# Attention and a mixture of experts: tokens sent to their two experts by indirect transfers, the experts' tiles computed inside the attention

## The chip, the cores and the metric

The kernel runs on one core of a Trainium2 chip. The metric is the device time of one execution in microseconds. The engines are PE (TensorE, with weight loads listed as PEld), DVE (VectorE), ACT (ScalarE), POOL (GpSimd) and SP (SyncE, which issues all DMAs of the kernel before). Each has its own instruction stream and they meet by semaphores.

## The reference, cut to what matters

The input x is 2 x 2048 tokens of 256 features, all float32. `xn = layernorm(x)`, and the output is `x + attention(xn) + experts(xn)`.

The attention has 16 heads of 16 features, rotary embedding of Q and K, a causal mask, softmax, and an output projection with a bias.

The experts: gate logits over 10 gates (8 true experts and 2 null ones), softmax, the two largest gates; of these the weights of true experts are divided by their sum; each expert is a 256 x 256 matrix with a bias:

```python
gate_probs = softmax(x @ gate_w.T + gate_b)
weights, selected = top_k(gate_probs, 2)
true_weights = weights * (selected < 8)
norm_w = true_weights / (true_weights.sum() or 1)
out = einsum('te,teh->th', combine_w, einsum('td,edh->teh', x, expert_w) + expert_b)
```

So a token needs at most two of the eight expert products.

## The kernel before, in words

`build` (L1495) calls three parts, each a block in which all engines run and at whose end they meet: `project`, `attend` and `output`. `acc` holds x, then the sums, for all 32 tiles of 128 tokens in SBUF.

**`project` (L61).** Eight steps of one chunk of 512 tokens each (two batches by four chunks, `s = 2 * j + b`). For each chunk DVE computes the statistics (`norm_a`, L388) and normalises (`norm_c`, L399); PE transposes the chunk (`transposes`, L655); ACT writes it as a float16 high half (`copy_xT`, L298) and DVE the low half (`low_x`, L408). Products then run in three float16 passes (high x high, high x low, low x high; `product`, L662). PE makes V and the gate logits (`values`), four blocks of Q and K (`queries`) and, for every token, all eight experts (`experts`, L703: 4 banks a tile, 6 matmuls of 512 columns each). DVE weighs and adds the expert products into `acc` (`combine`, L552). The gate (`gates_a`, `gates_b`, L497 and L507) is a chain of some 40 small DVE operations a chunk. Q and K blocks are copied by ACT (`copy_q`, L321), shuffled and multiplied by DVE (`rope`, L480), multiplied and added by POOL (L270, L272), and split in halves by ACT (`high`, L330) and POOL (`rest`, L275). SP stores V (4 DMAs) and Q and K (16 DMAs) of each chunk to scratch in HBM. Queues are in program order; the first chunk runs in float32 products, so that it need not wait for the split weights.

**`attend` (L777).** Eight groups of four heads (two loop turns unrolled into `r = 0, 1`). Before the first group, PE and DVE work through `first_items`, row maxima for two chunks. In a group there are 40 units (a chunk of 512 queries against a tile of 128 keys). For a unit PE makes scores of four heads in the three banks of psS (`scores`, L1358), ACT takes the exponential (L1215), POOL masks it where it is a diagonal unit (16 of the 40, L1186), and PE multiplies by V (`pv`, L1379). At most 4 units of probabilities are open. Beside this run "items" that use one of the two slots of psP in strict turn: "q", scores for the row maxima of later chunks, reduced by DVE (L1325, L1252); "m", the transposed maxima, which SP stores into Qs (`store_m`, L1105); "o", a chunk's output, transposed by PE (L1425) and normalised by DVE (`normalise`, L1257). The order of scores, items and products on PE is written out by `schedule` (L890), which simulates PE, ACT, DVE and POOL with fixed costs; the same order is used in all groups but the last, which has fewer items. All engines follow it strictly.

**`output` (L1435).** For each of 32 tiles PE transposes the attention's result and multiplies by Wout, ACT copies in between, DVE adds to `acc`, and SP stores 4 tiles at a time.

## Time and profile before

| | us |
|---|---|
| median of 3 runs | 1189.08 (1187.52 to 1189.19) |
| the profiled execution | 1192.72 |
| its span, first to last instruction | 1190.6 |
| PE busy | 1071.2 (90%) |
| DVE busy | 976.3 (82%) |
| ACT busy | 712.0 (60%) |
| POOL busy | 212.7 (18%) |
| mean granted TensorE clock | 0.941 |

The span is some 2 us shorter than the execution's time. Busy shares are means over the three parts, which have different limits; the rows below take them apart. Matmuls are pipelined and their ends modelled, so that a busy PE is not PE at its peak. The clock is a share of 2.4 GHz; its two levels are 1.0 and 0.5.

### The profile page before, as it was taken

To read this page: it belongs to the slowest core of one execution; us is meant where nothing else is said; L and a number is where in the kernel's file an instruction comes from. 1 tells how busy PE (TensorE), PEld (TensorE's weight loads), DVE (VectorE), ACT (ScalarE), POOL (GpSimd) and SP (SyncE) were. 2 spreads that over 40 slices of the span, in tenths; PEclk is the share of its full clock that TensorE was granted. 3 is DMA by queue.
4 is the path that set the end of the run, shared out by engine and by line. 5 is a ranking of instruction groups with operands and counts; after the bars stand their busy time and mean duration, and the time that the engine had idled before them with its cause. 6 is when DMAs were issued, how large, how long until landed. Compare 5 with 4: busy or idle time off the path is not lost. (4 is left out here: it accounts for less than half of the span.)

```text
span 1190.6 us, 25362 instructions
## 1 busy us (share of the span) xinstructions
PE 1071.2 (90%) x7800; PEld 416.2 (35%) x7800; DVE 976.3 (82%) x1610; ACT 712.0 (60%) x1545; POOL 212.7 (18%) x250
## 2 busy tenths in 40 slices
PE   4599899899965999999899999899999999999988
PEld 3244444444421332333323333233333233233247
DVE  6988788788859899999799899889989889989113
ACT  2333232332200688788588788678878868878752
POOL 2534254234510001001001101100100100110100
PEclk9799899899985799999899999989999999999889
DMA  8012122121230401101100200200110110000003
GB/s 292 25 56 80 36 74 67 53 88 36 64 85 13 99 2 45 47 2 46 48 2 11 81 2 2 71 22 3 45 46 2 45 47 2 2 2 2 1 18 124
DMA packets 50207, 53.37 MB, mean 45 GB/s; under 512 B 5201, under 2 KB 40602, under 8 KB 50074
## 3 DMA queue, kind: packets, MB, share of 16 engines
q1 hardware_dynamic: 50074, 51.75, 14.4%
q8 instruction: 65, 1.06, 0.4%
q14 instruction: 68, 0.56, 0.2%
HBM read 30.43 MB, written 20.97 MB: 43 GB/s over the span
## 5 line engine op out<-in xcount | busy, mean ns | idle before, releaser
L1215 ACT ACTIVATE probs<-psS 128x512 f32<-128x512 f32 (+3 forms) x1280 | 586.0, 541 | 216.8 <-PE psS L1367 207.4
L1252 DVE TENSOR_REDUCE blk<-psP 128x2 f32<-128x1024 f32 (+2 forms) x576 | 636.2, 1159 | 64.9 <-PE psP L1328 53.2
L1367 PE MATMUL psS<-Qs,Ks 50*128 50x512 f16 (+3 forms) x1280 | 347.5, 358 | 14.9 <-ACT probs L1215 9.0
L1325 PE MATMUL psP<-Ks,Qs 48*128 48x512 f16 (+3 forms) x1280 | 295.9, 368 | 43.3 <-DVE blk L1252 21.5
L1392 PE MATMUL psO<-probs,Vs 128*32 128x512 f32 (+3 forms) x2560 | 308.7, 554 | 1.4 <-ACT probs L1215 0.4
L1186 POOL TENSOR_SCALAR_AFFINE_SELECT probs<-probs 128x512 f32<-128x512 f32 x128 | 81.5, 636 | 711.7 <-ACT probs L1215 711.7
L666 PE MATMUL psM<-wp,xp 128*128 128x512 f16 x768 | 183.8, 391 | 15.8 <-DVE odd L571 9.8
L1367 PEld LDWEIGHTS psS<-Qs,Ks 50*128 50x128 f16 x1280 | 100.5, 95 | 258.5 <-ACT probs L1215 200.7
L1325 PEld LDWEIGHTS psP<-Ks,Qs 48*128 48x128 f16 x1280 | 74.9, 95 | 169.6 <-DVE blk L1252 128.3
L666 PEld LDWEIGHTS psM<-wp,xp 128*128 128x128 f16 x768 | 75.8, 101 | 111.8 <-issue 19.1
L1328 PE MATMUL psP<-later,eye 64*128 64x128 bf16 x1024 | 95.4, 231 | 0.0
L1392 PEld LDWEIGHTS psO<-probs,Vs 128*32 128x32 f32 x2560 | 51.8, 108 | 87.6 <-issue 73.9
L1328 PEld LDWEIGHTS psP<-later,eye 64*128 64x128 bf16 x1024 | 73.3, 102 | 18.6 <-issue 5.0
L270 POOL TENSOR_TENSOR swp<-swp,trig 128x512 f32<-128x512 f32 x32 | 42.5, 1327 | 180.7 <-DVE rot L486 180.7
L563 DVE SCALAR_TENSOR_TENSOR acc<-psM,cs,acc 128x256 f32 (+1 forms) x128 | 60.7, 474 | 14.1 <-PE psM L666 8.5
L334 ACT CAST part<-rot 128x512 f16<-128x512 f32 x32 | 19.0, 616 | 72.9 <-POOL rot L272 72.9
L1261 DVE RECIPROCAL rs<-psP 128x16 f32<-128x16 f32 x32 | 8.2, 257 | 51.9 <-PE psP L1425 51.9
L327 ACT ACTIVATE qs<-psQ 128x512 f32<-128x512 f32 x28 | 16.6, 593 | 57.2 <-PE psQ L666 57.2
L571 DVE SCALAR_TENSOR_TENSOR odd<-psM,cs,odd 128x256 f32<-128x256 f32 x96 | 45.3, 471 | 0.0
L272 POOL TENSOR_TENSOR rot<-rot,swp 128x512 f32<-128x512 f32 x32 | 41.6, 1300 | 2.5
L666 PE MATMUL psQ<-xp,wqp 128*128 128x512 f16 x168 | 40.9, 379 | 0.0
L277 POOL TENSOR_TENSOR part<-rot,part 128x512 f16<-128x512 f32 x32 | 39.7, 1248 | 6.5 <-ACT part L334 6.5
(115 smaller groups left out, 643.1 us busy)
## 6 DMA issues: line engine op xcount, KB each, us to landing
v_scratch<-vst SPq DMA_DIRECT2D x32, 256.0 KB, 3.2
qk_scratch<-part SPq DMA_DIRECT2D x128, 64.0 KB
Vs<-v_scratch SPq DMA_DIRECT2D x16, 512.0 KB, 4.5
acc<-x SPq DMA_DIRECT2D x8, 512.0 KB, 7.4
Ks<-qk_scratch SPq DMA_DIRECT2D x32, 128.0 KB, 2.7
Qs<-qk_scratch SPq DMA_DIRECT2D x32, 128.0 KB, 2.7
out<-acc SPq DMA_DIRECT2D x8, 512.0 KB, 2.9
we_sb<-we SPq DMA_DIRECT2D x8, 256.0 KB, 7.3
```

The lines of the kernel that those rows point to most:

```text
L270: step(nc.gpsimd.tensor_tensor(swp[k][:, :], swp[k][:, :], trig[:, 1, :], ALU.mult))
L272: nc.gpsimd.tensor_tensor(rot[k][:, :], rot[k][:, :], swp[k][:, :], ALU.add).then_inc(sum_ok[k], 1)
L563: nc.vector.scalar_tensor_tensor(out=rows, in0=psM[:, n, 0:D], scalar=cs[b][:, t, e:e + 1], in1=rows, op0=ALU.mult, op1=ALU.add).then_inc( ...
L571: ins = nc.vector.scalar_tensor_tensor(out=odd[t % 2][:, :], in0=psM[:, n, D:2 * D], scalar=cs[b][:, t, e + 1:e + 2], in1=odd[t % 2][:, :] ...
L666: ins = pe.matmul(out, lhs(x, w, k), rhs(x, w, k), start=(n == 0), stop=(n == len(todo) - 1))
L1186: nc.gpsimd.affine_select(out=v, in_=v, compare_op=ALU.is_ge, fill=0.0, base=0, pattern=[[0, HG], [1, P]], channel_multiplier=-1).then_inc ...
L1215: nc.scalar.activation(probs[u % NPR][:, h, q0:CH], psS[:, n % SB, q0:CH], ACT.Exp, scale=exp_scale).then_inc(s_read[n % SB], 1)
L1252: nc.vector.tensor_reduce(out, src, AX.X, ALU.max).then_inc(item_ok[slot], 1)
L1325: ins = pe.matmul(psP[:, slot, at:at + w], Qs[r][rows, qt // CT, p, t * P:(t + 1) * P], Ks[r][rows, kc, p, 0:w], start=True, stop=True)
L1328: ins = pe.matmul(psP[:, slot, at + w - P:at + w], eye[all_rows, i, :], later[all_rows, i, :], start=False, stop=True, skip_group_check=True)
L1367: pe.matmul(psS[:, n % SB, q0:CH], Ks[r][rows, kt // CT, p, kt % CT * P:(kt % CT + 1) * P], Qs[r][rows, c, p, q0:CH], start=True, stop=Tru ...
L1392: ins = pe.matmul(psO[h * VW:(h + 1) * VW, q0:CH], Vs[r][:, kt, h * VW:(h + 1) * VW], probs[u % NPR][:, h, q0:CH], start=(kt == 0), stop=e ...
```

## The change

**Projection.** The expert products, `combine` and the per-chunk gate are gone. All eight chunks now run one scheme: wait for the split weights, then `values`, `transposes` of the next chunk, four `queries` in two psQ banks. `xn` is kept for all 32 tiles. The low half of Q and K is computed by DVE (`split`) instead of POOL. SP, ahead of the stores, fills the scratch arrays `xs` (9984 rows of 256 float32) and the end of `ys` with zeros. After the last chunk the gate of all 4096 tokens is computed at once, with matmuls that count how many tokens go to each expert and where each token's row lies in a list sorted by expert and padded to tiles of 128; the weights of each expert are split and stored to `we_s`.

**Attention.** In groups 0 and 1 POOL sends the rows of `xn` to their two places in `xs`, two transfers after every mask. In groups 2 to 5 (`kind == "experts"`) nine pairs of tiles a group are worked as items "x" and "y" in the psP slots. In groups 6 and 7 POOL fetches the results from `ys` into `xn`, and DVE adds them, weighed, to `acc` in group 7.

**Output.** The expert biases and `bout` come in by one more product a tile, of a 54-row bf16 matrix of weights with a 54-row matrix of biases.

The core of the diff:

```diff
+            sp.dma_start(xs[:, :].rearrange("(n p i) d -> p n (i d)", p=P, i=2),
+                         zero[...].to_broadcast([P, TRASH // (2 * P) + 1, 2 * D])).then_inc(spare, 16)
...
+            def split(s, k):
+                dve.wait_ge(high_ok[k], ONE + s + 1)
+                nc.vector.tensor_tensor(part[k][:, 1, :], rot[k][:, :], part[k][:, 0, :], ALU.subtract
+                                        ).then_inc(split_ok[k], 1)
...
+            def body(j, start, last):            # DVE, projection
+                for b in range(NB):
+                    s = 2 * j + b
+                    if not (last and b == 1):
+                        low_x(s + 1, 1 - b)
+                    if not (start and b == 0):
+                        split(s - 1, 2)
+                    rope(s, j, 0)
+                    if not (start and b == 0):
+                        split(s - 1, 3)
+                    rope(s, j, 1)
+                    if not last:
+                        norm_a(s + 2, j + 1, b)
+                    rope(s, j, 2)
+                    split(s, 0)
+                    rope(s, j, 3)
+                    split(s, 1)
+                    if not last:
+                        norm_c(s + 2, j + 1, b)
...
+            for e in range(EXPERTS):             # ACT, after the loop; DVE follows with the low half
+                if e >= 2:
+                    act.wait_ge(e_stored[e % 2], ONE + 16 * (e // 2))
+                    act.wait_ge(el_ok, ONE + e - 1)
+                nc.scalar.activation(wep[e % 2][:, 0, :, :], we_sb[:, :, e * D:(e + 1) * D], ACT.Copy,
+                                     scale=wscale[:, OF_E:OF_E + 1]).then_inc(eh_ok, 1)
...
+        EG = MTILES_USED // 2 // 4               # 72 tiles, 9 pairs in each of four groups
+        def with_e(queue):
+            seq, every = list(queue), len(queue) // EG
+            for i in range(EG):
+                at = seq.index(queue[i * every + 2])
+                seq.insert(at, ("x", i))
+                seq.insert(at + 4, ("y", i))
+            return seq
...
+            def load_e(buf, n):                  # SP
+                sp.dma_start(xt[buf], xs[bass.ds(n * 2 * P, 2 * P), :]...).then_inc(e_in[buf], 16)
+                for i in range(2):
+                    e = sp.value_load(etab[0:1, bass.ds(n * 2 + i, 1)], min_val=0, max_val=EXPERTS - 1)
+                    sp.dma_start(wt[2 * buf + i], we_s[bass.ds(e, 1), :, :]...).then_inc(e_in[buf], 16)
...
+            def scatter(t, i):                   # POOL
+                if (t, i) != (0, 0):
+                    pool.wait_ge(scattered, 16 * (TILES * i + t))
+                nc.gpsimd.indirect_dma_start(out=xs[:, :], out_offset=bass.IndirectOffsetOnAxis(ap=idx[:, i, t:t + 1], axis=0),
+                                             in_=xn[:, t, :], in_offset=None).then_inc(scattered, 16)
+            for r in range(2):
+                for d, u in enumerate(masks):
+                    mask(0, r, u)
+                    for t in range(d * EACH, (d + 1) * EACH):
+                        scatter(t, r)
...
+            for d, u in enumerate(masks):
+                mask(3, 0, u)
+                for t in range(d * EACH, (d + 1) * EACH):
+                    gather(t, 0)
+            for d, u in enumerate(masks):
+                mask(3, 1, u)
+                for q in [q for q in range(QUARTERS) if SECOND[q] == d]:
+                    pool.wait_ge(added, ONE + q + 1)
+                    for t in range(q * QT, (q + 1) * QT):
+                        gather(t, 1)
...
+                        elif x[0] in "xy":       # ACT, in the order of the items
+                            if x[0] == "x":
+                                nc.scalar.activation(xT[buf][:, 0, :], psP[:, slot, 0:CH], ACT.Copy, scale=XSCALE
+                                                     ).then_inc(hi_ok, 1)
+                            else:
+                                act.wait_ge(y_stored[buf], ONE + 16 * before)
+                                nc.scalar.copy(yt[buf], psP[:, slot, 0:CH]).then_inc(item_ok[slot], 1)
...
+            def low(j, r, x, slot):              # DVE
+                dve.wait_ge(hi_ok, ONE + EG * (2 * (j - 1) + r) + x[1] + 1)
+                nc.vector.scalar_tensor_tensor(out=xT[buf][:, 1, :], in0=psP[:, slot, 0:CH], scalar=XSCALE,
+                                               in1=xT[buf][:, 0, :], op0=ALU.mult, op1=ALU.subtract
+                                               ).then_inc(item_ok[slot], 1)
+            def add(i, q):
+                dve.wait_ge(y_in[i][q], 16 * QT)
+                for t in range(q * QT, (q + 1) * QT):
+                    ins = nc.vector.scalar_tensor_tensor(out=acc[:, t, :], in0=xn[:, t, :], scalar=wsel[:, i, t:t + 1],
+                                                         in1=acc[:, t, :], op0=ALU.mult, op1=ALU.add)
...
+            def expert(buf, slot):               # PE, 12 matmuls of 256 columns
+                todo = [(w0, w1, k) for w0, w1 in ((0, 0), (0, 1), (1, 0)) for k in range(KC)]
+                for t in range(2):
+                    for n, (w0, w1, k) in enumerate(todo):
+                        ins = pe.matmul(psP[:, slot, t * D:(t + 1) * D], xT[buf][:, w0, at:at + P],
+                                        wt[2 * buf + t][:, of:of + D], start=(n == 0), stop=(n == len(todo) - 1))
...
+                pe.matmul(ps[:, t % 4, 0:D], cT[t % 2][:, :], b54[:, :], start=False, stop=True).then_inc(o_ps, 1)
```

## Rows read from the trace of the kernel before

**Rows 1.** Busy us of each engine by stretch, clock, DMA share, GB/s.

```profile
54.00:343.00 289.00, 260.76 (x1228) 123.96 (x1228) 241.55 (x708) 83.55 (x166) 107.54 (x87) 0.96 0.19 59
343.00:392.00 49.00, 25.12 (x147) 8.51 (x148) 39.26 (x43) 0.00 (x0) 3.69 (x14) 0.52 0.23 59
492.00:584.00 92.00, 85.40 (x757) 28.91 (x757) 82.11 (x93) 71.69 (x160) 10.06 (x16) 0.98 0.10 27
1050.00:1106.00 56.00, 53.33 (x476) 17.42 (x473) 49.75 (x59) 45.59 (x95) 4.46 (x7) 1.00 0.01 2
1106.00:1149.00 43.00, 37.48 (x242) 9.78 (x238) 1.88 (x7) 32.43 (x77) 6.36 (x10) 0.88 0.00 1
1149.00:1190.00 41.00, 36.83 (x192) 30.91 (x192) 13.96 (x33) 11.82 (x32) 0.00 (x0) 0.96 0.31 103
```

**Rows 2.** Timeline of POOL, masks of two groups: start us, us, operation, idle before.

```profile
399.85 0.64 POOL L1186 TENSOR_SCALAR_AFFINE_SELECT probs<-probs 128x512 f32<-128x512 f32 x1 [48.73 <-ACT probs L1215]
...
491.87 0.64 POOL L1186 TENSOR_SCALAR_AFFINE_SELECT probs<-probs 128x512 f32<-128x512 f32 x1 [10.70 <-ACT probs L1215]
...
551.70 0.64 POOL L1186 TENSOR_SCALAR_AFFINE_SELECT probs<-probs 128x512 f32<-128x512 f32 x1 [6.18 <-ACT probs L1215]
...
572.64 0.64 POOL L1186 TENSOR_SCALAR_AFFINE_SELECT probs<-probs 128x512 f32<-128x512 f32 x1 [3.17 <-ACT probs L1215]
```

**Rows 3.** Timeline of DVE and PE in the projection's loop.

```profile
175.88 1.40 DVE L392 BATCH_NORM_STATS2 stat<-acc 128x6 f32 x4
...
177.63 1.29 DVE L413 SCALAR_TENSOR_TENSOR xp<-xnT,xp 128x512 f16<-128x512 f32 x2
...
183.24 1.38 DVE L404 TENSOR_SCALAR xn<-acc,mv,rstd 128x256 f32 x4
...
186.97 0.73 DVE L485 STREAM_SHUFFLE swp<-qs 128x512 f32<-128x512 f32 x1
187.60 0.67 DVE L486 TENSOR_TENSOR rot<-qs,trig 128x512 f32<-128x512 f32 x1
...
301.98 1.46 PE L666 MATMUL psQ<-xp,wqp 128*128 128x512 f16 x6
```

**Rows 4.** POOL's first rotation (timeline) and ACT's high halves (groups of instructions).

```profile
27.87 1.26 POOL L270 TENSOR_TENSOR swp<-swp,trig 128x512 f32<-128x512 f32 x1 [17.50 <-DVE rot L486]
...
L334 ACT CAST part<-rot 128x512 f16<-128x512 f32 x29 | 17.3, 616 | 67.1 <-POOL rot L272 67.1
```

**Rows 5.** Timeline: one DVE product beside POOL and without it.

```profile
40.70 1.15 POOL L277 TENSOR_TENSOR part<-rot,part 128x512 f16<-128x512 f32 x1 [5.05 <-ACT part L334]
...
40.72 1.18 DVE L545 TENSOR_TENSOR c<-cw,den 128x32 f32<-128x32 f32 x1
...
202.44 0.19 DVE L545 TENSOR_TENSOR c<-cw,den 128x32 f32<-128x32 f32 x1
```

**Rows 6.** V stores, issue and landing (min/median/max), and the loads' rate (by stretch).

```profile
L212 SPq DMA_DIRECT2D v_scratch<-vst x32: 372/417/1441, 21.0 to 300.5; - x32
...
DMA to landing us min/median/max: 2.5/3.2/5.3
...
14.00:16.00 2.00, 2.00 (x8) 1.89 (x9) 1.90 (x9) 1.11 (x3) 0.00 (x0) 1.00 1.09 384
```

**Rows 7.** Timeline of DVE in the opening: maxima and low halves of expert weights.

```profile
19.77 4.47 DVE L444 TENSOR_REDUCE whalf<-we_sb 128x2 f32<-128x2048 f32 x2
...
32.10 4.75 DVE L470 SCALAR_TENSOR_TENSOR wp<-we_sb,wscale,wp 128x512 f16<-128x512 f32 x4
```

**Rows 8.** Timeline of DVE and PE inside group 1.

```profile
551.89 4.62 DVE L1252 TENSOR_REDUCE blk<-psP 128x2 f32<-128x1024 f32 x4 [0.22 <-PE psP L1325]
...
555.98 0.65 PE L1425 MATMUL psP<-identf,ot 128*128 128x128 f32 x4
...
565.10 0.26 DVE L1261 RECIPROCAL rs<-psP 128x16 f32<-128x16 f32 x1 [0.81 <-PE psP L1425]
...
574.53 0.43 PE L1392 MATMUL psO<-probs,Vs 128*32 128x128 f32 x8
```

1170 lines of the change are left out of this document (651 added, 519 removed).

## The prediction

> **What bounds the kernel now.** I read the busy time by stretch first. It splits the 1190.6 us span into projection (0 to 343), the attention's opening (343 to 392), eight groups, and the output stage from 1149 [rows 1]. In the projection's loop PE is busy 261 of 289 us and DVE 242: both hold the pace, and ACT (84) and POOL (108) do not. A steady attention group lasts 92.0 us, the distance of its first mask from that of the group before [rows 2]. In it PE is busy 85 to 89, DVE 82, ACT 72, POOL 10. So the projection has two engines near their limit, and the change takes most of the work off both. The groups have PE and DVE near the limit and ACT behind them, and the change puts work on all three. In the last 43 us of attention DVE is all but idle (1.9 busy).
>
> **The projection, from 343 us to what.** Removed are 32 x 4 expert products of 6 matmuls, the DVE sums that follow them, and 8 chains of small gate operations. What is left per chunk on DVE, by the starts in the rows, which overlap a little [rows 3]: the x split 1.2, statistics 1.75, reciprocal and normalise 0.2 + 1.4, four shuffles of 0.63 and four rotary products of 0.6 (4.9), and now also four low halves taken over from POOL, priced as the rotary product, 2.4. Sum 11.9 us. PE: 24 value products of 266 columns, 24 query products of 512 (1.46 us for six, [rows 3]) and 8 transposes, about 10 us. ACT: 4 query copies of 0.6, 4 high halves of 0.616 [rows 4], two x halves and three V and gate copies, about 8. POOL: 8 products of 1.26 [rows 4], 10.1.
>
> DVE is then the longest, but not alone. Two things add. First, the last DVE operation of a chunk (normalise for the chunk after next) is followed by PE transposes (0.6 for the first half), the ACT half (0.6) and two handovers before DVE can go on: 1.5 idle. Second, DVE and POOL can't both read SBUF pairs: the same 128x32 product took 0.19 us with POOL idle and 1.18 beside a POOL subtraction of 1.15 that began 0.02 before it [rows 5]. Eight such DVE operations meet eight POOL operations in each chunk; laying them out one after another gives about 3 us more. I take 16.5 us a chunk. Ends: 14 (no collisions) and 20.
> The Trainium skill's page "SBUF — State Buffer" (section "SBUF: two separate sides") says the pair of ports shared by VectorE and GpSimd is an exclusive lock, taken by a DVE operation with two SBUF inputs for its whole length against a GpSimd operation. By that rule the chunk is 16.5, without it 13.5, 20 us less over the loop; the two rows agree with the rule.
>
> POOL's first rotation starts at 27.9 [rows 4], so DVE began the first shuffle at 26.5. Now the weights' three halves are made first on ACT and DVE (about 2.1 more after overlap) and the value and query products run in three fp16 passes, perhaps at the lower clock (4.4 more): 33 us. Then a fill of scratch with zeros is queued before the first stores: 9984 rows of 1 KB and 768 more, 11.0 MB. The loads reached 384 GB/s [rows 6], say 350: the 9.2 MB of loads end at 28, the fill at 60. The stores of chunk 0 are behind it and land there plus about 3; part[0] is wanted again at 33 + 16.5 + 5 = 55. Stall 8 us (0 to 20). Six chunks of 16.5 and one without normalisation (13) bring the last chunk's first product to 33 + 8 + 99 + 13 = 153, its end (POOL's four rotations) to 168.
>
> Behind the loop stands a serial tail that nothing covers. Gate: 17 operations on 256 or 320 elements per partition, 0.42 to 0.5 each by scaling from the rotary product, about 8; 20 small ones of 0.2, 4; the maxima of the expert weights 4.5 [rows 7] and 0.6; two low halves 1.3; scales 1; waits for 32 counting matmuls and then 33 more at half clock, 4; places and tile table 6.5. Sum 30. Then eight weight splits through two buffers: DVE 1.2 each [rows 7], issue and landing of the 256 KB store 3.2 [rows 6], ACT 0.65 and handovers, 5.9 for each pair of experts, 24 for four. 168 + 54 = 222. The projection gives back 343 - 222 = **121 us** (ends 105 and 140). The attention's opening stays 49.
>
> **Groups 2 to 5: 36 pairs of tiles, nine a group.** A pair is an item "x" (4 transposes, ACT high half, DVE low half) and an item "y" (12 matmuls, ACT copy). Both take one of two psP slots that alternate strictly with the score reductions, 1.15 us each on DVE (four in 4.62, [rows 8]). PE: 0.6 for the transposes (0.65 for four, [rows 8]), and 12 x 256 columns are the columns of the six in rows 3, 1.3 to 1.46; 1.95 x 9 = 17.6 us. DVE: 0.69 of work (the x split's half, [rows 3]), and idleness: in "x" the slot passes 0.65 + 0.6 + handovers and ACT's queue (ACT is 78% busy) while DVE has only 1.15 in the other slot, so 1.0 idle; in "y" DVE sees neither slot for 1.46 + 0.6 - 1.15 and then waits again for the refill, 1.4. Nearest row: DVE stood 0.81 idle ahead of an "o" item, which has no ACT step inside it [rows 8]. 3.1 x 9 = 28 us on DVE, of which its present 10 us of idleness may take some. Below: 14 (both hide in each other); above: 33 (PE's strict order adds waits). I take 23, between PE's 17.6 and DVE's 28: 4 x 23 = **+92** (56 to 132). The transfers, 1 MB a pair, need 3 us of every 12.8 at 350 GB/s; hidden. SP's waits for "y" stand in front of mask-row and next-group loads, but these are wanted several items later.
>
> **Groups 0 and 1: scatters.** After each mask POOL issues two indirect transfers, each waiting until the one before has landed. Queued behind them is the next mask, and for that waits psO's product on PE and all behind it. No row shows an indirect transfer. Landing of a 256 KB store, issue included: 2.5 to 5.3, median 3.2 [rows 6]; an issue costs SP 0.42 to 1.44 [rows 6], and for POOL I take the length of its product, 1.26. Mask, landing and second issue: 0.64 + 3.2 + 1.26 = 5.1 us (ends 0.64 + 2.5 + 0.42 = 3.6 and 0.64 + 5.3 + 1.44 = 7.4). The last eight masks of a group span 20.9 us [rows 2]: 7 x 5.1 - 20.9 = 14.8 late, less the 1.3 between a mask's end and its product [rows 2, 8]: 13 a group, **+26** (6 to 70; at 7.4 the masks ahead of these are late too).
> The Trainium skill's "DMA: Bandwidth & Descriptors" (section "Anatomy of one DMA — SWDGE (gpsimd) path") gives 2.0 us plus bytes over 436 GB/s for a transfer issued by GpSimd, 2.3 here; by it the step would be 4.2 us and the sum for both groups 14 instead of 26. No row here shows it.
>
> **Groups 6 and 7: gathers and sums.** In group 6 the gathers wait for nothing: 0.64 + 2 x 1.26 = 3.2 a mask, 7 x 3.2 is 22, nothing late. In group 7 four bursts of eight hold POOL 10 us each, and 32 DVE sums of 0.4 (by size from the rotary product; 12.8) fall into a stretch in which DVE is busy 50 of 56 us [rows 1]; the other 32 lie where it is idle. **+12** (3 to 30).
>
> **Output.** 32 tiles are 192 matmuls in 36.8 us of PE, almost all of the 41 [rows 1]. One bf16 transpose and one 256-column product more, with their weight loads: 0.25 x 32 = **+8** (4 to 12); the added ACT copy fits.
>
> **Sum.** -121 + 92 + 26 + 12 + 8 = +17. The profiled execution took 1192.7 us beside its span of 1190.6, so it becomes 1210; the median before is 1189.1, so the forecast is **1206 us**.
>
> **Rivals.** *Experts mostly hidden, faster.* No stall by the fill (-129), a group gains only 17 (PE's own addition: 68), scatters 10, gathers 6, output 6: -39, 1150 us. For it: PE's busy time in rows 1 counts latencies that overlap, and DVE has 10 us idle. Against: two slots only, strict order. 0.31. *POOL is the bound in groups 0 and 1 and in 7*: step 7.4, scatters 70, gathers 30: +79, 1268. It decides from a step of about 5.5 us on. 0.07. *The projection's loop goes at half clock*: PE would sit idle a third of each chunk, and in the attention's opening, with PE busy 25 of 49 us, the granted clock was 0.52, near its lower level of 1.2 GHz [rows 1]; against: in the groups, PE busy 85 of 92, it was 0.98, and in the old loop 0.96. Then PE needs 5.3 + 10.2 + 2 = 17.5 a chunk inside the chain, period 21.5, +37: 1243. 0.09. *The expert part waits for something not priced* (its loads or SP's order): 1260, 0.03. The forecast itself, 1190 to 1230: 0.50.
>
> **Chances.** Faster by over 0.2%: 0.31 and 0.05 of the forecast's low side, 0.36. Within 0.2% (what a measurement of this kernel can tell from no change): 0.05. Slower: 0.59. The range 1148 to 1247 leaves out POOL's case, the unpriced wait and half of the tail below the first rival.
>
> **What would show it.** The first attention mask at about 279 us instead of 400 (right projection); 16.5 us between chunks' first rotary products; groups 2 to 5 at 115 us, with DVE idle ahead of "x" halves and after "y"; groups 0 and 1 at 105 us with PE waiting for POOL in the last eight masks. Wrong if groups 2 to 5 stay under 107, if the loop needs over 20 us a chunk, or if scatters cost POOL under 4 us a mask.

## The result, and the profile after

The changed kernel takes 1295.1 us (median of 4 runs, 1292.8 to 1297.8) against 1189.1 of the kernel before in the same job: ratio 1.088, 95% interval 1.084 to 1.093. Forecast were 1206 and a range up to 1247. Slower was right as the likelier side; the size was wrong, and it was too small in every term of the groups and the output. Of the 83 us between the forecast's +17 and the span's +100, 24 lie in groups 2 to 5, 24 in group 7, 12 in groups 0 and 1, 10 in the output, 6 in group 6 and 7 ahead of the first mask.

The profiled execution spans 1291.0 us instead of 1190.6. The first view to read is again busy time by stretch (us of the stretch; busy us and instructions of PE, weight loads, DVE, ACT, POOL; granted clock; DMA share; GB/s). The stretches here are the projection's loop, its tail, the attention's opening, group 0, group 4 up to its last mask and from there to group 5's first, group 7, and the output:

```profile
0.00:187.00 187.00, 91.49 (x454) 54.06 (x454) 134.18 (x262) 58.16 (x116) 102.78 (x89) 0.78 0.58 194
187.00:231.00 44.00, 6.58 (x68) 5.95 (x68) 30.66 (x67) 9.43 (x13) 0.00 (x0) 0.58 0.22 78
231.00:285.50 54.50, 33.05 (x202) 12.15 (x204) 43.68 (x48) 4.57 (x9) 4.08 (x16) 0.50 0.29 77
285.53:395.70 110.17, 96.25 (x792) 30.96 (x790) 85.20 (x97) 75.45 (x165) 41.37 (x49) 0.88 0.22 71
762.14:859.76 97.62, 94.33 (x790) 36.17 (x786) 72.30 (x79) 75.83 (x167) 9.52 (x15) 0.98 0.31 91
859.76:885.96 26.20, 20.64 (x154) 10.02 (x146) 19.75 (x27) 8.56 (x16) 0.64 (x2) 0.65 0.46 132
1108.64:1231.44 122.80, 97.03 (x595) 24.13 (x595) 66.41 (x111) 71.50 (x156) 40.88 (x48) 0.76 0.12 35
1231.44:1291.00 59.56, 55.03 (x256) 35.16 (x256) 14.01 (x33) 16.87 (x64) 0.00 (x0) 0.94 0.21 71
```

The projection gave back what it should. The last stretches are what [rows 1] had at 105 (last group) and 41 (output): the output now takes 59.6 and PE is busy in 55 of them, the last group 122.8 at clock 0.76.

The masks on POOL mark the groups, as in [rows 2] (start us, us, operation, idle before and what ended it). Two steps of group 1's late masks stand among them:

```profile
285.53 0.63 POOL L1280 TENSOR_SCALAR_AFFINE_SELECT probs<-probs 128x512 f32<-128x512 f32 x1 [48.85 <-ACT probs L1343]
395.70 0.63 POOL L1280 TENSOR_SCALAR_AFFINE_SELECT probs<-probs 128x512 f32<-128x512 f32 x1 [5.61 <-ACT probs L1343]
...
482.45 0.96 POOL L1288 DMA_INDIRECT sent_scratch<-xn,idx  x1 [1.70 <-DMA sent_scratch<-xn,idx]
483.43 0.64 POOL L1280 TENSOR_SCALAR_AFFINE_SELECT probs<-probs 128x512 f32<-128x512 f32 x1
485.11 0.97 POOL L1288 DMA_INDIRECT sent_scratch<-xn,idx  x1 [1.04 <-DMA sent_scratch<-xn,idx]
487.78 0.96 POOL L1288 DMA_INDIRECT sent_scratch<-xn,idx  x1 [1.70 <-ACT probs L1343]
488.76 0.64 POOL L1280 TENSOR_SCALAR_AFFINE_SELECT probs<-probs 128x512 f32<-128x512 f32 x1
...
513.97 0.63 POOL L1280 TENSOR_SCALAR_AFFINE_SELECT probs<-probs 128x512 f32<-128x512 f32 x1 [12.67 <-ACT probs L1343]
```

The step from mask to mask is 5.33 us (483.43 to 488.76): two issues of 0.96, and before each a wait until the scatter before has landed. Issue and landing are 0.96 + 1.70 = 2.66, the step is two of these, and the mask lies inside the first landing. First masks of the eight groups, and the last normalisation, give the ledger:

| stretch | before | after | difference | forecast |
|---|---|---|---|---|
| to the first mask | 399.9 | 285.5 | -114 | -121 |
| groups 0 and 1 | 190.2 | 228.4 | +38 | +26 |
| groups 2 to 5 | 380.5 | 496.9 | +116 | +92 |
| group 6 | 91.6 | 97.8 | +6 | 0 |
| group 7 to its last normalisation | 86.7 | 122.8 | +36 | +12 |
| output | 41.6 | 59.6 | +18 | +8 |
| sum | 1190.6 | 1291.0 | +100 | +17 |

Before, groups took 92.0, 98.2, 93.2, 98.2, 93.4, 95.7 and 91.6: "a steady group lasts 92.0" was one group of [rows 2], 2.6 under their mean. Groups 1 and 3 are the long ones (98.2): PE stands there for 4.3 and 4.2 us on nothing that the profile names, once ahead of the first turn of the attention's loop and once between its two turns. The stand of group 3:

```profile
773.85 0.28 PE L1325 MATMUL psP<-Ks,Qs 48*128 48x128 f16 x1 [4.15 <-issue]
```

### The profile page after: what moved, and what is told of

Read it like the earlier page. It is cut to its first block and busy times, and to the rows that moved or that the text cites. A ratio compares the mean times of both kernels' runs of the same rounds, so it can differ in the third digit from the quotient of the medians.

```text
span 1291.0 us, 24075 instructions
## 1 busy us (share of the span) xinstructions
PE 1025.9 (79%) x7658; PEld 407.1 (32%) x7658; DVE 912.9 (71%) x1228; ACT 724.3 (56%) x1576; POOL 311.3 (24%) x361
## 3 DMA queue, kind: packets, MB, share of 16 engines
q1 hardware_dynamic: 87238, 104.22, 26.2%
q8 instruction: 66, 1.08, 0.4%
## 5 line engine op out<-in xcount | busy, mean ns | idle before, releaser
L1547 PE MATMUL psS<-Qs,Ks 50*128 50x512 f16 (+3 forms) x1280 | 349.3, 376 | 18.2 <-ACT probs L1343 8.2
L1591 PE MATMUL psO<-probs,Vs 128*32 128x512 f32 (+3 forms) x2560 | 325.8, 583 | 44.1 <-POOL probs L1280 41.3
L1505 PEld LDWEIGHTS psP<-Ks,Qs 48*128 48x128 f16 x1280 | 77.1, 98 | 198.8 <-DVE blk L1401 98.2
L1288 POOL DMA_INDIRECT sent_scratch<-xn,idx x64 | 62.2, 971 | 87.7 <-DMA sent_scratch<-xn,idx 77.0
L694 PE MATMUL psT<-ident,xn 128*128 128x128 f32 x64 | 14.8, 408 | 73.4 <-DVE xn L447 60.6
L1292 POOL DMA_INDIRECT xn<-expert_scratch,idx x64 | 60.6, 946 | 17.2 <-issue 16.1
L1569 PE MATMUL psP<-xn 128*128 128x256 f16 x432 | 58.1, 288 | 3.0 <-DVE blk L1401 2.4
L702 PE MATMUL psQ<-xp,wqp 128*128 128x512 f16 x192 | 52.7, 438 | 4.7 <-ACT qs L360 4.6
L1434 DVE SCALAR_TENSOR_TENSOR xn<-psP,xn 128x512 f16<-128x512 f32 x36 | 24.9, 692 | 43.4 <-ACT xn L1361 43.4
L1444 DVE SCALAR_TENSOR_TENSOR acc<-xn,wsel,acc 128x256 f32<-128x256 f32 x64 | 26.8, 490 | 33.1 <-DMA xn<-expert_scratch,idx 33.1
L1365 ACT COPY xn<-psP 128x512 f32<-128x512 f32 x36 | 21.1, 585 | 50.9 <-PE psP L1569 50.9
L1569 PEld LDWEIGHTS psP<-xn 128*128 128x128 f16 x432 | 41.6, 102 | 21.5 <-issue 14.7
```

The source lines that it names most:

```text
L702: ins = pe.matmul(out, lhs(x, w, k), rhs(x, w, k), start=(n == 0), stop=(n == len(todo) - 1))
L1288: nc.gpsimd.indirect_dma_start(out=xs[:, :], out_offset=bass.IndirectOffsetOnAxis(ap=idx[:, i, t:t + 1], axis=0), in_=xn[:, t, :], in_offs ...
L1292: nc.gpsimd.indirect_dma_start(out=xn[:, t, :], out_offset=None, in_=ys[:, :], in_offset=bass.IndirectOffsetOnAxis(ap=idx[:, i, t:t + 1], ...
L1505: ins = pe.matmul(psP[:, slot, at:at + w], Qs[r][rows, qt // CT, p, t * P:(t + 1) * P], Ks[r][rows, kc, p, 0:w], start=True, stop=True)
L1547: pe.matmul(psS[:, n % SB, q0:CH], Ks[r][rows, kt // CT, p, kt % CT * P:(kt % CT + 1) * P], Qs[r][rows, c, p, q0:CH], start=True, stop=Tru ...
L1569: ins = pe.matmul(psP[:, slot, t * D:(t + 1) * D], xT[buf][:, w0, at:at + P], wt[2 * buf + t][:, of:of + D], start=(n == 0), stop=(n == le ...
```

## The experiments

Each is a version of the changed kernel, but for the eighth. Times are medians of 4 to 10 runs (two in the fifteenth) against 1295.1 (and 1189.1 before); group lengths are from the masks of one profiled execution of each. The experiments ran in five jobs, in which the kernel before took 1187.0 to 1190.8, so a few microseconds between medians of different jobs mean nothing. Code is condensed to the lines that matter.

One thing has to be known to read the totals. Twelve of these kernels (the changed one and experiments 1, 2, 4, 5, 6, 9, 10, 12, 13, 14 and 16) have the same group 7 and output stage, but for the array from which four of them (1, 12, 13, 14) gather, and yet the time from group 7's first mask to the end is 176.6 to 182.4 us in seven of them and 185.6 to 192.7 in the five others. Those five (1, 2, 4, 9 and 10) are the ones in which VectorE stands there twice, 7.3 us in all, and PE 11 to 17 us in all, on nothing that the profile names; in the seven no such stop is recorded. Whether every execution of such a kernel has these stops is not on record.

**1. Are the pairs the whole loss of groups 2 to 5?** Without the x and y items:

```
-            if kind == "experts":
-                queue = with_e(queue)
```


> The changed kernel without the 36 x and 36 y items in groups 2 to 5, and so without their loads and stores; the gathers read the tokens as they were sent, since no expert's output exists. The median of the changed kernel was 1295.1 us, and its groups 2 to 5 took 123.4 to 124.9 us each where the old kernel's took 93.2 to 98.2 (497 against 381 in all). Theory A, the two items are the whole loss there: the groups fall back to 93 to 98 and the kernel to 1295 - 116 = 1179 (1172 to 1187). Theory B, a part of the loss is that something else makes the new groups slower (the larger program, the buffers that lie elsewhere, a lower clock left from groups 0 and 1): groups stay at 100 or more, the kernel above 1195.

1176.8 us. Groups 2 to 5 took 378.3, as before the change. Theory A; the pairs cost 118 us, by the medians and by the groups (119). The profiled execution, 1187.1, was the slowest of the four.

**2. Scatters in GpSimd's idle time.**

```
+            for _ in range(14): scatter(*next(sends))     # ahead of the first mask
             for r in range(2): for d, u in enumerate(masks):
                     mask(0, r, u)
-                    for t in range(d * EACH, (d + 1) * EACH): scatter(t, r)
+                    for _ in range((3,2,3,4,1,2,2,2,0,0,0,1,0,1,0,4)[d]): scatter(*next(sends))
```


> The same 64 scatters, each still waiting for the landing of the one before, but placed where GpSimd is idle: 14 before the first mask, and after the sixteen masks of groups 0 and 1 3, 2, 3, 4, 1, 2, 2, 2, 0, 0, 0, 1, 0, 1, 0, 4 instead of two after each (a step from one issue to the next is 2.68 us). Theory A, the masks of groups 0 and 1 are late because they queue behind the scatters on GpSimd: the two groups take 94 to 100 instead of 110 and 118, the kernel 1265 (1257 to 1275). Theory B, the transfers themselves are in the way (traffic, or GpSimd's writing of descriptors against VectorE's use of its port), wherever they are issued: groups 0 and 1 keep 105 or more, the kernel stays at 1285 or above.

1273.9 us. Groups 0 and 1 took 197.6 instead of 228.4, 7 above their time before the change, with all 64 scatters still there. Theory A: it was the masks' place in the queue. Of these 31 us the kernel kept 21: groups 2 to 5 were 3 us longer, group 6 two, and the stretch from group 7 on, with the stops described above, 3.

**3. Group 7 without bursts, the second expert in the output stage.**

```
-                for q in [q for q in range(QUARTERS) if SECOND[q] == d]: ... gather(t, 1)
     # output stage, POOL: 32 gathers; DVE, four tiles behind its own addition:
+                acc[:, u, :] = xn[:, u, :] * wsel[:, 1, u] + acc[:, u, :]
```


> Group 7 without its four bursts of eight gathers and with the sums of the first expert at its last items, where VectorE is idle; the gathers of the second expert are issued in the output stage and its 32 sums stand there too, behind the output's own additions. In the changed kernel the time from group 7's first mask to the last normalisation was 122.8 us, before the change 86.7. Theory A, the loss of 36 us is the sums in the first half of the group (15 us by the seventh mask) and the bursts that stand ahead of masks (19 us from there on): group 7 takes 87 to 93, the output stage gains at most 3, the kernel is at 1295 - 31 = 1264 (1258 to 1270). Theory B, most of it is PE's lower clock in this stage (0.76 against 0.95), which would stay: under 12 us come back, the kernel is above 1283.

1299.9 us, a miss for both theories. Group 7 fell from 122.8 to 93.6, so theory A holds there; but the output stage went from 59.6 to 94.3. Its timeline while POOL issued its gathers:

```profile
1223.03 0.42 DVE L1710 TENSOR_TENSOR acc<-ps,acc 128x256 f32<-128x256 f32 x1 [2.00 <-PE ps L1688]
...
1232.17 0.42 DVE L1710 TENSOR_TENSOR acc<-ps,acc 128x256 f32<-128x256 f32 x1 [8.72 <-remote]
...
1237.08 0.26 ACT L1697 COPY cT<-psT_c 54x128 bf16<-54x128 bf16 x1 [10.72 <-remote]
...
1248.98 0.42 DVE L1710 TENSOR_TENSOR acc<-ps,acc 128x256 f32<-128x256 f32 x1 [15.99 <-issue]
...
1255.28 0.26 ACT L1697 COPY cT<-psT_c 54x128 bf16<-54x128 bf16 x1 [17.68 <-remote]
```

ScalarE stands 17.7 us ahead of a copy that waits for no gather. The stops end with the gathers: the last is issued at 1251.2, and from 1260.9 on sums and additions run at 1.62 us a tile. Between 1228 and 1260 no packet of the instruction queues is recorded, so a late load of code does not show either.

**4. The projection's normalisation earlier.**

```
                     split(s, 0)
+                    norm_c(s + 2, j + 1, b)
                     rope(s, j, 3)
                     split(s, 1)
-                    norm_c(s + 2, j + 1, b)
```


> The projection's loop with the normalisation of the chunk after next before the fourth rotation instead of last in the chunk, and ScalarE's square root for it one query copy earlier. The loop's period was 20.3 us where 16.5 were forecast; PE stood 9.3 us before each chunk's transposes, VectorE idled 4.2. Theory A, the surplus is the chain normalise, transpose, halves, queries, rotation, which nothing covers at the chunk's edge: with the normalisation earlier the period falls to 16 to 17.5 and the kernel to 1295 - 7 x 3.3 = 1272 (1265 to 1280). Theory B, VectorE's own work, made longer by GpSimd's use of the shared port, is the bound: the period stays above 19, the kernel above 1286.

1289.3 us, above theory A's 1280 for the kernel. The period fell from 20.3 to 17.0 and the first mask came 16.2 us earlier: theory A for the loop, to 0.5 us of the forecast's 16.5. But the kernel gained 6. Groups 0 to 6 were 2 us longer, and from group 7's first mask to the end it took 192.1 us instead of 182.4. In that group DVE stood 2.5 and 4.8 us and PE 4.0 and 5.0 on nothing that the profile names, the first three of them during bursts of gathers (1134 to 1144, 1165 to 1175). Experiments 1, 2 and 9, with the projection as it was, have the same stops, so the earlier normalisation is not what brings them.

**5. A thin y item,** 2 of 12 products (5/6 of the experts' products left out):

```
-                todo = [(w0, w1, k) for w0, w1 in ((0, 0), (0, 1), (1, 0)) for k in range(KC)]
+                todo = [(0, 0, 0)]
```


> The changed kernel with 2 of the 12 expert matmuls in each y item (the experts' products are left out but for one sixth); all items, slots, waits, copies, loads and stores stay. The 36 pairs cost 116 us with the 12 matmuls (1.47 us an item). Theory A, TensorE's own time is the price (20.8 us of the pairs a group, in a group where PE is busy 115 of 124): 36 x 1.25 = 45 go, the groups take 112 to 114, the kernel 1250 (1242 to 1258). Theory B, the price is the passage of the two slots through ScalarE and VectorE, and PE's share is mostly covered: under 20 us go, the kernel stays above 1275.

1268.6 us, between the theories: groups 2 to 5 took 474.6, 22 less, for 45 us of PE time taken away (in group 4 PE was busy 103.5 instead of 115.0 us and the group lasted 7.0 less). In this order of work half of the PE time taken away comes back.

**6. VectorE out of the pairs** (slot freed by ScalarE's half, low half not made; the products that would read it read the high half, so PE makes the same 12):

```
-                                                     ).then_inc(hi_ok, 1)
+                                                     ).then_inc(item_ok[slot], 1)
```


> VectorE is taken out of the pairs: the x item's slot is freed by ScalarE's high half, the low half is not made (the six products that would use it take the high half instead, so PE does the same 12 matmuls). VectorE loses 0.69 of work and 1.0 of idleness in front of it per pair. Theory A (PE sets the pace of groups 2 to 5): at most 0.4 a pair, the kernel at 1280 to 1290. Theory B (VectorE sets it, as 28 of the forecast's terms had it): 36 x 1.7 = 61, the kernel at 1234 (up to 1250).

1290.7 us, and groups 2 to 5 took 497.1 against 496.9. DVE had 5 us less of work in group 4 and nothing came of it in the groups. Theory B, the larger of the forecast's two costs, is out.

**7. The second expert's rows in buffers of their own.**

```
+        ADDS = {2: [(0, 0)], NL - 3: [(0, 1), (0, 2), (0, 3)], NL - 2: [(1, 1), (1, 2)], NL - 1: [(1, 3), (1, 0)]}
+        FIRST = (4, 3, 4, 5, 2, 2, 2, 3, 0, 0, 0, 2, 0, 1, 1, 3)     # gathers after each mask, group 6
+        SECOND = (3, 3, 3, 3, 3, 3, 3, 3, 2, 2, 1, 1, 1, 1, 0, 0)    # and group 7
+        own = [Qs[0], Ks[0], Vs[0]]                                  # as 24 rows of 256
```


> Second attempt at group 7: the second expert's rows are gathered into buffers of their own (the free query, key and value buffers of the even groups; 8 tiles reuse the first rows), one to three after a mask, no burst and none in the output stage; all sums but the first eight stand behind the last reductions. In the attempt with the gathers in the output stage group 7 fell from 122.8 to 93.6 us, but there all engines stood still up to 18 us while the gathers ran. Theory A, sums and bursts are the loss of group 7, and gathers hurt other engines only where these run through new code without pause: group 6 at 92 to 96, group 7 at 90 to 97, output 60, the kernel at 1265 (1258 to 1272). Theory B, the gathers slow whatever runs beside them: group 7 above 105, the kernel above 1275.

1265.9 us. Group 6 took 91.9, group 7 99.2 (1108.85 to 1208.0), output 57. Theory A, with group 7 two us above its bound.

**8. Gathers beside the output stage of the kernel before,** read by nobody:

```
+            for t in range(TILES): indirect_dma_start(out=taken[:, t, :], in_=rows, in_offset=picks)
```


> The kernel before the change with 32 gathers of 128 rows by GpSimd in its output stage, whose data nobody reads and nobody waits for until the end (32 x 1.25 = 40 us of issues beside a stage of 41). Theory A, indirect transfers in flight hold back the loading of other engines' code, which this stage needs since its 32 tiles are written out: PE, ScalarE and VectorE stand still for 5 to 18 us at a time, the stage grows by 20 to 40, the kernel to 1210 to 1230. Theory B, the stop was a wait of the new sums on their data: nothing stands still, the kernel ends with the last landing, at most 8 us later, 1190 to 1197.

1193.5 us against 1188.4 in the same job (ratio 1.004, interval 1.002 to 1.006). No engine stood still: the additions kept their 1.08 us a tile. Theory B as to the time; theory A, that gathers in flight hold other engines' code, is not borne out.

**9. The pairs' groups in another order.**

```
-    pick = "s" if early or act < dve - (300 if more else 0) else "i"
+    pick = "s" if early or act < dve - (2500 if kind == "experts" else 300 if more else 0) else "i"
+    HOLD, DVE_DUE = 500, 1200      # experts; and y six items behind x
```


> The same instructions in groups 2 to 5 in another order: the list takes an item wherever one is ready (VectorE counted as due 1200 instead of 600 ns later, holds of 500 instead of 200 ns, y six instead of four items behind its x), so that about 5 instead of 24 items are left when the group's last scores and PV products are done. In the changed kernel such a group has 101 us in which PE is busy 97 of them (VectorE 75) and then 23 us of items alone, in which PE's granted clock is 0.50 to 0.63; before the change this end was 12.7 us. Theory C, the work is in the wrong places: PE is the limit first and the two slots are after it, so each group gives back most of the 10 us more at its end and the kernel falls to 1255 (1240 to 1270), groups to 111 to 116. Theory A, PE's total of work sets the group wherever the items stand: groups stay at 120 or more, the kernel above 1280.

1298.8 us, groups 2 to 5 at 491.0, 122.8 each, as theory A has it; the total is high because the end of the kernel has the stops. Theory C fails: with the items spread evenly the first part of group 4 grew from 97.6 to 101.6 and its end shrank only from 26.2 to 22.4.

**10. The normalisation on ScalarE,** on top of the fourth:

```
-   nc.vector.tensor_scalar(out, tile, mean, rstd, ALU.subtract, ALU.mult)
+   nc.scalar.activation(out, tile, ACT.Identity, bias=shift, scale=rstd)
```


> On top of the earlier normalisation (period 17.0 us, median 1289.3) the normalisation itself goes from VectorE to ScalarE, as x times 1/deviation plus a shift; VectorE keeps the reciprocal and a small product. The four normalisations took VectorE 3.04 us a chunk beside GpSimd. Theory A, VectorE is the loop's bound with 15.4 of 17.0 busy: the period falls to 14.3 to 14.8, the first mask comes 16 to 19 us earlier than with the normalisation early alone (269.3), the kernel at 1272. Theory B, the chain over GpSimd's two products per rotation (11.2 busy and waits on rotations) or PE (11.0 at clock 0.80) takes its place: period above 16, kernel above 1283.

1290.5 us; the period was 17.2 (17.0 in the fourth). Theory B: PE now stands 6.0 us on ScalarE's normalisation where it stood 5.95 on VectorE's. Taking the normalisation's 3 us off VectorE did not shorten the period, so VectorE's load alone does not set it; the chain through PE, ScalarE and GpSimd is what is left, and it was not cut further.

**11. Experiments 2, 4, 7 and 9 together.**

> The four rearrangements together: scatters where GpSimd is idle, earlier normalisation, second expert's rows in buffers of their own with the sums at the end, and the even order of groups 2 to 5. Alone the first three gave 21, 6 and 29 us. If the losses are separate they add: with 40 for the order 1295 - 96 = 1199 (1185 to 1220), above or at the 1188 of the kernel before. If they share a cause (the code loads, or a clock that falls when anything is idle) the sum is smaller: above 1225.

1235.2 us, a miss: 1199 was forecast with 40 for the order, and groups 2 to 5 kept 490.6, as in the ninth. The four together gave 60, where 21, 6 and 29 were the gains of the other three alone. In the profile 15 us were gained at the first mask, 27 in groups 0 and 1, 6 in groups 2 to 5 and 21 from group 7 on, and 7 were lost in group 6 (105.2, with the same gathers as the seventh's 91.9). So what the earlier normalisation gives at the first mask is not lost again in group 7, where the bursts of gathers are gone.

**12. The order alone:** laid out for the pairs, the pairs then left out.

```
-        orders = {kind: schedule(kind) for kind in KINDS}
+        orders = {kind: [x for x in schedule(kind) if x[0] not in "xy"] for kind in KINDS}
```


> Groups 2 to 5 in the order made for the pairs, but with every x and y item (and their loads and stores) left out of it. With the order of the plain groups and no pairs the kernel takes 1177 us and these groups 93 to 98. Theory D, the order itself (PE's strict list, laid out around pairs) is a part of the price: groups at 100 or more, the kernel above 1200. Theory E, the order costs nothing by itself: groups at 93 to 99, the kernel 1177 to 1184.

1228.1 us: with the plain order and no pairs 1176.8. The groups took 441.4 against 378.3, so the order costs 63 us in the groups; in the medians it is 51, and the profiled executions differ the other way outside these groups (experiment 1's end has stops, this one's has none). Theory D so far. Group 4 in two parts, up to the last mask and from there on, first in experiment 1, then here:

```profile
702.74:783.48 80.74, 78.80 (x680) 25.67 (x679) 75.46 (x82) 67.80 (x152) 9.55 (x15) 0.99 0.06 18
783.48:796.07 12.59, 11.38 (x111) 4.74 (x113) 9.34 (x16) 6.98 (x14) 0.64 (x1) 0.86 0.37 107
```
```profile
728.67:817.57 88.90, 82.69 (x666) 25.20 (x662) 67.52 (x72) 67.73 (x152) 9.55 (x16) 0.96 0.06 17
817.57:839.13 21.56, 16.62 (x134) 7.20 (x126) 18.44 (x25) 6.89 (x13) 0.64 (x2) 0.67 0.20 62
```

VectorE's work has slid behind the last mask (82 and 16 instructions against 72 and 25), where little else is left, PE idles and its clock is 0.67.

**13. No loads and stores for the pairs** (all work on the first two pairs' data).

> All x and y items run, but on the first two pairs' data: the 1 MB of loads and stores per pair and SP's waits for y are left out. Theory F, they matter (SP's waits in front of the mask rows, for which the next chunk's scores wait, and traffic 0.34 of the DMA engines): at least 15 us come back, the kernel below 1280. Theory G, as forecast, they are hidden: 1290 to 1297.

1288.2 us, between the bounds of the two theories (1280 and 1290); groups 2 to 5 at 494.6. The groups speak for theory G: 2 us in 497.

**14. Also 8 of 9 y items a group left out.**

> As without the transfers, and also 8 of the 9 y items a group left out, in the same order. The y items' PE time is 1.6 us each, the x items' 0.7. Theory A', each item costs about its PE time and a fixed passage: by the 26 us that ten twelfths of y gave (0.74 an item), y's whole price is 32 x 1.3 to 1.8 = 42 to 58 and the kernel ends 42 to 58 below the one without transfers; x then carries the remaining 50 to 60, 1.5 an item with 0.7 of PE. If y carries nearly all (over 80), it is its hold on a slot (PE and ScalarE one after the other, 2.1 us, while VectorE waits), and x is cheap.

1260.5 us, groups 462.6: 32 us for 32 y items, 1.0 each with 1.6 of PE time, less than the 42 to 58 forecast. Against the twelfth, 36 x and 4 y items cost 21 us in the groups, where 50 to 60 were expected for x. In the kernel's own order the pairs' 119 us are then 63 for the order, 21, 32 and 2 for the transfers.

**15. The third again without its sums.**

> The third experiment again (second expert's gathers in the output stage), but with its 32 sums on VectorE left out, so that no engine waits for the gathers; only the end waits for their landing. There the stage took 94 us with standstills of 8 to 18 us on PE, ScalarE and VectorE. If the gathers hold the engines up, the standstills stay and the stage takes over 80; if the sums' waits did it, the stage takes 60 and the kernel ends at 1262 to 1268.

1266.4 us; the last normalisation at 1201.6 and the span 1264.1 leave 62 for the output, and no engine stood still once the stage had begun (1.62 us a tile throughout). So the gathers alone did not bring the standstill: it takes the 32 sums behind them, with which the output's stores also come later. How ScalarE and PE came to stand longer than any wait on those sums explains stays open.

**16. The plain order with the pairs put into it.**

```
+        orders["experts"] = between(orders["plain"])   # x before every 8th reduction item, y 4 behind
```


> Groups 2 to 5 in the plain groups' order with the x and y items put into it at even distances (x before every eighth reduction item, y four such items behind it), instead of the order laid out with them. Theory D, the order is a price of its own, 51 us: what stays is transfers 7, y items 31, x items 29, so 1177 + 67 = 1244 (1236 to 1256), groups at 109 to 113, and the stretch from the last mask to the next group's first back at 14 to 18 instead of 26. Theory H, the plain order with pairs in it makes PE wait in its strict list for slots as the planner's tried to avoid: groups stay at 120 or more, the kernel above 1285.

1284.1 us, and the groups took 487.0 (forecast about 444 by theory D). Theory D fails, and theory H has the numbers almost right (121.8 a group for 120 or more, 1284 for above 1285) but not the reason: PE's idleness is the smaller part, as group 4 shows. The reading that fits is that the order's 63 us were mostly holes made for the pairs, which the pairs fill, and that without holes the pairs' PE time is paid almost in full. Groups 3 and 4 here, each in two parts:

```profile
640.92:748.29 107.37, 100.71 (x823) 38.48 (x823) 81.43 (x90) 78.60 (x169) 9.51 (x15) 0.97 0.33 92
748.29:768.66 20.37, 14.02 (x115) 6.47 (x116) 10.19 (x17) 7.72 (x15) 0.64 (x2) 0.69 0.42 121
768.66:873.28 104.62, 98.09 (x823) 38.49 (x821) 81.89 (x90) 78.55 (x169) 9.51 (x16) 1.00 0.34 95
873.28:887.20 13.92, 10.64 (x114) 4.80 (x114) 9.88 (x17) 7.61 (x15) 0.64 (x2) 1.00 0.62 172
```

At clock 1.00 a group is 118.5 us with PE busy 108.7. Without pairs it is 93.3 with 90.2 busy. So 18.5 of the 25.2 are PE's own time and 6.7 its idleness in the strict list. Group 3 has the same work and took 127.7. After its last mask PE stood 2.7 us for a mask row (1.9 in group 4), and then 3.4 us where the loop turns, which group 4 does not have:

```profile
755.37 0.60 PE L1559 MATMUL psS<-Qs,Ks 50*128 50x512 f16 x3 [2.68 <-DMA Qs<-nmT]
...
760.30 0.28 PE L1517 MATMUL psP<-Ks,Qs 48*128 48x128 f16 x1 [3.38 <-issue]
```

The granted clock was 1.00 up to 756, 0.50 from 758 on and for the rest of the group.

**17. The sixteenth with 2, 4 and 7.**

> The plain order with the pairs, scatters where GpSimd is idle (21), the earlier normalisation (6) and the second expert's rows in buffers of their own (29) together. If the losses are separate: 1244 - 56 = 1188 (1178 to 1200), level with the kernel before (1188). With the planner's even order the four together gave 60 where 52 was the sum of their parts, so a little better than the sum can be. If the order gives nothing: 1235.

1212.0 us, 24 above the forecast's 1188, since the order gave 11 us and not 51. The ratio to before is 1.020 (1.018 to 1.022): the best version that keeps all the work, and still slower. Its span is 1210.2. Against the kernel before: 130 less to the first mask, 10 more in groups 0 and 1, 111 in groups 2 to 5, 0 in group 6, 28 from there to the end.

## Why the prediction was wrong, point by point

**Projection: right, -114 for -121, by errors that met, which is luck.** The loop ended at 187 instead of 168, the tail took 44 instead of 54, and the stretch behind it to the first mask 54.5 instead of 57. GpSimd's first rotary product came at 33.1 (forecast 33), the stall behind the zero fill is the 25.5 instead of 20.2 us between the second and the third chunk's, 5.3 (8 forecast; ScalarE waits 9.2 us there for chunk 0's stores), the last chunk had 13.7 (13). The step that was off is the period: 20.3 instead of 16.5. The chain was named, but only ACT's half and handovers were counted in it; its chief part is the wait of PE's strict list for the normalisation, the last thing VectorE does:

```profile
109.37 3.04 DVE L447 TENSOR_SCALAR xn<-acc,mv,rstd  x4
...
112.46 1.97 PE L694 MATMUL psT<-ident,xn 128*128 128x128 f32 x8 [9.29 <-DVE xn L447]
113.61 0.60 ACT L343 ACTIVATE xp<-psT 128x512 f16<-128x512 f32 x1 [7.04 <-PE psT L694]
...
117.69 0.72 DVE L517 STREAM_SHUFFLE swp<-qs 128x512 f32<-128x512 f32 x1
...
119.28 1.45 POOL L322 TENSOR_TENSOR swp<-swp,trig 128x512 f32<-128x512 f32 x1 [7.67 <-DVE rot L518]
```

PE waits 9.3 us, then the queries (ready only after the transposes) start, and rotations wait for them. Experiment 4 shows it.

The cost of VectorE and GpSimd working side by side is there: the four normalisations take 3.04 beside GpSimd against 1.38 alone [rows 3], and the rotary product 1.12 against 0.67. The Trainium skill's "SBUF — State Buffer", section "SBUF: two separate sides", says that the shared pair is an exclusive lock for the whole instruction, against a VectorE operation with two SBUF inputs or in a two-port mode. The product's rows agree; the normalisation has one large input and pays too, which only the second case would cover, and no run here shows its mode. In the tail the eight weight splits took 12.2 us (213.2 to 225.4), not 24, because a pair of experts passed in 3.6 us, landing included.

**Groups 2 to 5: the step that failed is "28 us on DVE", from which the value of 23 a group was taken.** Experiment 6 takes VectorE out and the groups gain nothing. What the runs show in its place is TensorE's time and the order of its list, 29 us a group. By its busy time in group 4 of the changed kernel the four transposes are 0.70 a pair and the twelve products 1.6, together 20.8 a group instead of 17.6:

```profile
L1569 PE MATMUL psP<-xn 128*128 128x256 f16 x108 | 14.5, 289 | 0.7 <-DVE blk L1401 0.6
...
L1561 PE MATMUL psP<-identf,xn 128*128 128x128 f32 x36 | 6.3, 301 | 0.6 <-DVE blk L1401 0.5
```

A part of that is the clock, 0.91 in this group. In experiment 16's group 4, at clock 1.00, they are 19.1:

```profile
L1581 PE MATMUL psP<-xn 128*128 128x256 f16 x108 | 13.3, 273 | 0.0
...
L1573 PE MATMUL psP<-identf,xn 128*128 128x128 f32 x36 | 5.8, 285 | 0.0
```

PE's 90.2 busy us of a group without pairs become 108.7 there, so all but 0.6 of the 19.1 is added. The other lines lie beside each other in time: in experiment 1's group 4 their own busy times add up to 134 us in 90 us of busy PE. The scores have 50 rows, the reduction products 48 and PV 32 columns, while the pairs' instructions have 128 by 128; that this is the reason is read from the shapes, and no run tests it. To PE's time come 6.7 us of idleness in the strict list (experiment 16) and, in the changed kernel's own order, the end of the group: 26.2 us from the last mask to the next group's first, at clock 0.65, against 12.6 at 0.86 in experiment 1. How much of the 29 us is PE's time and how much the order has no single answer: with the plain order it is 18.5 of 25.2, with the kernel's own order taking 45 us of PE time away gave back 22 (experiment 5). The forecast priced items; it never asked at which clock, nor what the order leaves for the end. That the transfers are hidden was right (experiment 13).

**Groups 0 and 1: mechanism right, size off, and the step right by luck.** Masks in the last eight are late by the queue, as forecast; measured +38 for +26. The step was 5.33 (forecast 5.1), but not for the reason given: the forecast's mask, one landing and one issue are 0.64 + 2.66 + 0.96 = 4.26 with the measured sizes, and it left out the wait of 1.04 before the first scatter, whose predecessor has not landed yet. Sizes taken too large made up for the wait left out. Each of the two groups lost 18 to 20 rather than 13: in group 0 the ninth mask was 0.4 late and the last 18.5 (99.2 us after the first against 80.7). The seven steps between took 39.1 instead of 35.7, one of them 7.35, and the 1.3 that the forecast took off again was not there to take: the next group began 18.2 late. The page "DMA: Bandwidth & Descriptors" of the Trainium skill (section "Anatomy of one DMA — SWDGE (gpsimd) path") says 2.0 us plus bytes over 436 GB/s for a transfer issued by GpSimd, by estimate 2.3 here; the rows have it landed 1.70 after an issue of 0.96, 2.66 in all. The 4.2 worked out from it missed for the same omitted wait.

**Group 6: not nothing but 6,** and with the gathers moved to GpSimd's idle time nothing (91.9 us in experiments 7 and 17; why it was 105.2 in experiment 11 is open).

**Group 7: the step that failed is +12.** Thirty-two sums of 0.41 stood in its first half where DVE has no room, as said, and masks were 15 us late by the fourth, ahead of this group's first burst. The first burst made no mask later. The other three did: the forecast let each hold POOL 10 us without asking for whom, and here a mask starts with no idle time right behind the eighth gather, with PE waiting for it:

```profile
1167.08 3.26 DVE L1444 SCALAR_TENSOR_TENSOR acc<-xn,wsel,acc 128x256 f32<-128x256 f32 x8
1170.25 0.20 DVE L1404 COPY nmT<-psP 32x128 f16<-32x128 f16 x1
...
1170.98 0.95 POOL L1292 DMA_INDIRECT xn<-expert_scratch,idx  x1 [0.16 <-issue]
...
1179.74 0.95 POOL L1292 DMA_INDIRECT xn<-expert_scratch,idx  x1 [0.30 <-issue]
1180.69 0.65 POOL L1280 TENSOR_SCALAR_AFFINE_SELECT probs<-probs 128x512 f32<-128x512 f32 x1
...
1181.39 0.56 PE L1591 MATMUL psO<-probs,Vs 128*32 128x128 f32 x8 [3.93 <-POOL probs L1280]
...
1182.53 3.25 DVE L1444 SCALAR_TENSOR_TENSOR acc<-xn,wsel,acc 128x256 f32<-128x256 f32 x8 [12.07 <-DMA xn<-expert_scratch,idx]
```

In this group PE waited 14.0 us for masks, in three waits of up to 5.7, one behind each of these bursts, and the granted clock was 0.76, so that what it did took longer. The sum at 1167.08 also stands in front of the mask row's copy, on which the last chunk's scores hang. Experiments 3 and 7 give back 29 and 24 of the 36; both move the sums and the bursts at once, so the two parts, 15 and 19 by the masks, were not tested apart.

**Output: sized wrong, 0.53 a tile instead of 0.25.** The additions to the output come every 1.62 us instead of every 1.08:

```profile
L1690 PE MATMUL ps<-b,cT 54*128 54x256 bf16 x32 | 9.2, 286 | 0.0
...
L1676 PE MATMUL psT_c<-identb,c 128*54 128x128 bf16 x32 | 7.8, 244 | 1.1 <-PEq L764 1.1
```

0.29 and 0.24 are 0.53, all serial on PE; the step that failed is the forecast's 0.25 for the two together, about half.

**Rivals.** "Experts mostly hidden" had it that PE's busy time overlaps: the pairs' products did the opposite. "POOL is the bound" named the right stages (38 and 36 us) and decided, it said, from a step of 5.5; the step was 5.33, and it bound all the same. "The projection's loop goes at half clock" (period 21.5) was partly so: the granted clock from 33 to 187 us was 0.74, and the period 20.3. But experiment 4 brought the period to 17.0 with the clock at 0.77, so the chain was the price and not the clock. "The expert part waits for something not priced" is answered by experiment 13: its loads and stores cost 2 us.

## What to carry to other kernels

Work moved from one stage into another is paid there in time of the engine that is full: read which engine that is in that stage (PE was busy 94.3 of 97.6 us here), whether its present work overlaps itself while the new work does not, and what the new order of its list costs even with the new work left out (63 us here). On an in-order queue ask of each added instruction which later one is already late; 64 scatters cost 38 us behind masks and 7 in the gaps. A gain in an early stage shows in the total only if no later stage loses time of its own, as in the five kernels with stops in group 7, so measure such edits by the mark they move as well as by the median.

## What the runs showed of the hardware that was not expected

- Two groups with the same work took 118.5 us, with the granted clock at 1.00 throughout, and 127.7 (experiment 16). In the longer one PE stood 2.7 and 3.4 us within eight microseconds, the clock fell to 0.50 between the two and stayed there to the group's end, and its last stretch took 20.4 us with PE busy 14.0 instead of 13.9 with 10.6. So that end is longer both by the time PE stands and by the slower clock.
- An indirect gather of 128 rows of 1 KB is issued every 1.25 us (0.95 busy, 0.30 between), and 32 in a row beside the output stage disturbed nobody (experiments 8 and 15); with sums behind them on VectorE, engines that wait for neither stood up to 17.7 us (experiment 3). Bursts of eight inside group 7 came with stops of up to 6.4 us on PE in five of twelve kernels with the same group 7, and with none in the changed kernel and six others. What links them was not found.
